# A fused MoE, attention, MoE block on one core: indirect transfers issued without waiting for the pair before, and all engine orders planned anew

## The chip, the cores and the metric

The kernel runs on one core of a Trainium2 chip. The metric is the device time in microseconds (us), taken over several runs. A profile of one execution stands beside it. Its engines are PE (TensorE, matrix products; PEld is its weight load), ACT (ScalarE), DVE (VectorE), POOL (GpSimd) and SP (SyncE, which only issues transfers). An "idle before" in a row is the time in which that engine did nothing ahead of the instruction, with what ended it.

## The reference

The input x has 16 batches of 512 tokens with 128 features, in float32. Three layers follow one another, each on the layer-normalised x and each added to x:

```
x = x + 0.5 * ffn(layernorm(x))     # stage A
x = x + attention(layernorm(x))     # stage B
x = x + 0.5 * ffn(layernorm(x))     # stage C, same weights as A
```

`ffn` is a mixture of 8 experts (128 to 256 to 128, relu between); each token takes its 2 best experts by softmax and adds their results with their softmax weights. `attention` has 8 heads of 32 features, with keys and values through a latent of 64, and a softmax over all 512 tokens of a batch.

## The kernel before

**Stages and steps.** The work is cut into small steps, named by (stage, index, name, number): for example `("C", 12, "xg", 0)`. In stage B the index is a batch, in A and C a batch or a chunk. A chunk is a group of one to three batches that are routed together: chunks 0 to 6 belong to stage A, 7 to 13 to stage C. Chunk 0 (batch 0) and chunk 13 (batch 15) are dense: every expert is computed for every token (`dh`, `dy`), so nothing has to be moved. The other twelve are routed:

- `norm`, `scaled`, `xTf`, `logits`: layer norm, transpose and gate products of a batch; `top1`, `top2`, `rank1`, `gate`, `rank2` choose the experts and compute each token's slot (`pos`, cast on VectorE at L1451).
- `scat` (L1076, GpSimd): for each tile of 128 tokens two indirect transfers, a pair, write the tile's rows to its two slots in DRAM (`slots_A`, `slots_C`). A chunk of three batches has 12 pairs.
- `xload`, `wload` (SyncE) fetch the slots by four tiles (a quad) and each tile's expert weights; `xg` (TensorE, L1657) transposes, `h` and `y` multiply, `ystore` writes to `results`.
- `gat` (L1096, GpSimd): for each tile a pair of indirect transfers brings the two results of every token to `Y`, which has room for two batches; `comb` (VectorE, L1467) adds them to X.

Stage B has for each batch `xT`, `q`, `k`, `v`, and for each of two groups of heads: `rmax` (scores for the maximum and the sums; PE, VectorE L1502, ScalarE L1177), `rsplit`, `mrow`, `s` (transposed scores; ScalarE's exponential at L1168), `pv`; then `wo` adds to X (L1487).

**What sets the order.** Every engine walks a fixed list of steps, in order, and waits at each for the semaphores it needs; a step that waits holds up all that stands behind it on its engine. The lists come from a planner that runs when the program is built (`all_steps`, `plan`): it plays the steps through with a table of costs and picks, whenever an engine is free, the possible step with the smallest due time. The due times are made from a table of numbers (`WANTED`, `B_SHIFT`, `A_SHIFT`, `C_SHIFT` and others). `GAP` is the least distance that the planner puts between the starts of two pairs on GpSimd:

```python
            if step.name in ("scat", "gat") and now < indirect + GAP:
                return False
```

**The wait between pairs.** Before each pair, `apart` waits until the pair ahead of it on GpSimd, scatter or gather, has landed in full. At most one pair is in flight. Besides that, the first scatter of a chunk waits for its slot numbers and for the loads of the chunk before; the first gather of a chunk for the last two stores of results; the first gather of a batch for the combine that frees its half of Y.

The end of the kernel is the routed chunk 12 (batch 14, four pairs out and four back, four quads) beside the dense chunk 13 (batch 15), then the stores of the last batches.

Of the kernel before, what the change touches and what calls it, by code (L numbers as in the profile page):

```python
# [16 lines left out]
TILES, HEADS, GROUP = 4, 8, 4  # L17
# [10 lines left out]
FIRST = tuple(sum(CHUNKS[CHUNKS_OF[s][0]:c]) for s in "AC" for c in CHUNKS_OF[s])  # L28
# [4 lines left out]
W_QUADS, XS_RING, XG_RING, HG_RING, YS_RING, Y_RING, XN_RING, XF_RING, C_RING = 2, 3, 2, 4, 2, 2, 4, 1, 3  # L33
# [10 lines left out]
def n_quads(c):  # L44
    return (n_tiles(c) + 3) // 4
# [36 lines left out]
def split_name(b, g):  # L82
# [4 lines left out]

PERIOD, FIRST_B = 57.89, 143.5  # L90
WANTED = {"norm": -84.66, "scaled": -16.08, "xT": -29.15, ("q", 0): -18.58, ("k", 0): -15.2, ("v", 0): 9.95,
          ("v", 1): -5.64, ("q", 1): 3.68, ("k", 1): 1.22, "wo": 66.92}
GROUP_GAP, MAX_PACE, S_FIRST, S_PACE, PV, ADD, SUM = 18.01, 2.93, 22.06, 0.27, -0.13, -1.26, 4.47
A_LEAD, A_PACE, A_ROUTE, A_NORMS = 40.59, 15.14, 36.72, 8.29
C_NORM, C_ROUTE, C_FIRST, C_PACE, C_GATHER = 63.2, 31.04, 20.92, 29.32, 52.0
LOAD_AHEAD, W_AHEAD = -3.49, -1.76
B_SHIFT = [86.54, -31.84, 6.54, 20.12, -49.35, 18.57, -78.69, -20.22, -54.3, 17.32, 4.45, 0.95, 4.94, -11.17, 16.45, 5.24]
A_SHIFT = [-41.32, -20.34, -9.8, -16.34, 14.33, 47.38, 30.34]
C_SHIFT = [10.17, 7.16, -58.43, 37.75, 10.94, -60.54, 5.88]
GAP = 4.4  # L100


def wanted_attention(b):
# [582 lines left out]
def macaron_kernel(nc, x, wq, wkv_down, wk_up, wv_up, wo, gate_w, gate_b, w1, b1, w2, b2, out):  # L686
# [17 lines left out]
    order = all_steps()  # L704
# [15 lines left out]
    comb_turn = {batch: i for i, batch in enumerate(combs)}  # L720
# [7 lines left out]
    with ExitStack() as ctx:  # L728
# [85 lines left out]
        gy_in = [sem(f"gy_in{i}") for i in range(Y_RING)]  # L814
# [58 lines left out]
        def scattered(s, b):  # L873
            return 32 * TILES * len([old for old in range(b % XN_RING, b + 1, XN_RING) if CHUNK_OF[s][old] != DENSE[s]])
# [11 lines left out]
        def ring_count(i, ring, each=16):  # L886
            return each * (i // ring + 1)
# [114 lines left out]
        def _(pool):  # L1002
# [42 lines left out]
                pool.tensor_tensor(pairs[:, kt // 2, j, :], probs[:, kt - 1, j, :], probs[:, kt, j, :],  # L1045
                                   ALU.add).then_inc(S["p_added"], 1)

            before = {step: old for old, step in zip(order["POOL"], order["POOL"][1:])}

            def apart(at):  # L1050


                old = before.get(at.step)
                if old and old[2] == "scat":
                    s, c, t = old[0], old[1], old[3]
                    b = FIRST[c] + t // TILES
                    pool.wait_ge(scat_in[s][b % XN_RING], scattered(s, b) - 32 * (TILES - 1 - t % TILES))
                if old and old[2] == "gat":
                    i = comb_turn[old[:2]]
                    pool.wait_ge(gy_in[i % Y_RING], ring_count(i, Y_RING, 32 * TILES) - 32 * (TILES - 1 - old[3]))  # L1060

            def scat(at):

                s, c, t = at.stage, at.index, at.k
                apart(at)
                if t == 0:
                    pool.wait_ge(S["pos_done"], at.count("pos_done", "rank2", 0))
                    if c == routed_chunks(s)[0]:
                        pool.wait_ge(zero_in[s], 16)
                    else:  # L1070
                        for q in range(max(0, n_quads(c - 1) - XS_RING), n_quads(c - 1)):
                            i = quad_turn[s, c - 1, q]
                            pool.wait_ge(xs_in[i % XS_RING], ring_count(i, XS_RING))
                b = FIRST[c] + t // TILES
                for k in range(2):
                    pool.indirect_dma_start(out=slots[s][:], out_offset=bass.IndirectOffsetOnAxis(ap=pos[s, c % C_RING][:, k, t:t + 1], axis=0),  # L1076
                                            in_=xn[s][:, xn_place(s, b) + t % TILES, :], in_offset=None).then_inc(
                        scat_in[s][b % XN_RING], 16)

            def gat(at):  # L1080

                s, b, n = at.stage, at.index, at.k
                c = CHUNK_OF[s][b]
                i = comb_turn[s, b]
                apart(at)
                if n == 0:
                    if b == FIRST[c]:
                        for q in range(max(0, n_quads(c) - YS_RING), n_quads(c)):
                            j = quad_turn[s, c, q]
                            pool.wait_ge(y_out[j % YS_RING], ring_count(j, YS_RING))  # L1090
                    if i >= Y_RING:
                        s0, b0 = combs[i - Y_RING]
                        pool.wait_ge(S["comb_done"], counts["comb_done", (s0, b0, "comb", 0)])
                t = (b - FIRST[c]) * TILES + n
                for k in range(2):
                    pool.indirect_dma_start(out=Y[:, i % Y_RING, k, n, :], out_offset=None, in_=results[s, c][:],  # L1096
                                            in_offset=bass.IndirectOffsetOnAxis(ap=pos[s, c % C_RING][:, k, t:t + 1], axis=0)).then_inc(
                        gy_in[i % Y_RING], 16)
# [730 lines left out]
```

## Time and profile before

| | |
|---|---|
| median of 3 runs | 1338.11 us (1331.24 to 1339.2) |
| span of the profiled execution | 1336.0 us |
| its time outside the span | not given by the profile |
| TensorE busy | 1227.4 us |
| ScalarE busy | 962.6 us |
| VectorE busy | 690.4 us |
| GpSimd busy | 470.8 us |

The span goes from the first to the last instruction of that execution, and all times in rows count from its start. A busy time leaves out everything in which an engine waits, whatever it waits for. For GpSimd it holds the time in which it makes the transfers' descriptors, not their flight.

### The profile page before, as it was taken

How to read it: one execution, taken by the hardware profiler on the slowest of the kernel's cores; microseconds unless marked ns; L12 is line 12 of the kernel's file. 1: busy time of each engine (PE TensorE's matmuls, PEld its weight loads, DVE VectorE, ACT ScalarE, POOL GpSimd, SP SyncE). 2: the span in 40 equal slices, each digit the busy share in tenths (PEclk: the TensorE clock that was granted, in tenths of full speed). 3: DMA queues.
4: the chain of work that ended last, by engine and by line, in shares of the span. 5: the costliest groups of instructions: out<-in, count | busy, mean ns of one | idle time of the engine just before them, and what ended most of it. 6: DMA issues, size and time to landing. Idle time of an engine off the chain costs nothing.

```text
span 1336.0 us, 25776 instructions
## 1 busy us (share of the span) xinstructions
PE 1227.4 (92%) x8269; PEld 811.4 (61%) x8269; DVE 690.4 (52%) x2239; ACT 962.6 (72%) x2383; POOL 470.8 (35%) x528
## 2 busy tenths in 40 slices
PE   6989888989999999999999899999799999998795
PEld 2676575576566557666657566667555457665474
DVE  4356446375675446356555365535547546454133
ACT  3338659578788887888887778886778788786331
POOL 2012424434344534234444343433334430243333
PEclk9978999899989998898989989999997879999898
DMA  7305472564645176556445536577421034645672
GB/s 255 141 13 172 145 218 85 175 197 141 190 146 163 48 222 182 160 154 188 132 145 166 150 99 206 166 215 215 147 72 47 31 120 150 195 151 151 206 227 65
DMA packets 159849, 202.04 MB, mean 151 GB/s; under 512 B 16922, under 2 KB 103394, under 8 KB 159715
## 3 DMA queue, kind: packets, MB, share of 16 engines
q1 hardware_dynamic: 144196, 168.90, 41.0%
q0 software_dynamic: 15360, 31.49, 8.1%
q8 instruction: 68, 1.11, 0.4%
q14 instruction: 65, 0.53, 0.1%
q10 hardware_dynamic: 160, 0.01, 0.0%
HBM read 152.49 MB, written 47.84 MB: 150 GB/s over the span
## 4 chain that ended last, share of the span: by engine, by line
DMA 35%; PE 26%; issue 14%; POOL 14%; ACT 7%; DVE 5%; SPq 0%; POOLq 0%; DVEq 0%; ACTq 0%
PE psum L1548 24%; DMA Y<-results_C,posC 10%; DMA slots_C<-xnC,posC 10%; DMA Y<-results_A,posA 8%; POOL Y L1096 7%; DMA slots_A<-xnA,posA 7%; POOL slots_C L1076 4%; ACT psum L1177 2%; POOL slots_A L1076 2%; ACT probs L1168 2%; DVE neg_m L1502 1%; DVE X L1467 1%; ACT xnA L1133 1%; PE psum L1657 1%; PE psum L1625 1%
## 5 line engine op out<-in xcount | busy, mean ns | idle before, releaser
L1548 PE MATMUL psum<-nat 32*128 32x512 f32 x2048 | 413.3, 674 | 17.0 <-ACT psum L1177 8.3
L1502 DVE TENSOR_REDUCE neg_m<-psum 128x1 f32<-128x512 f32 x512 | 318.2, 683 | 202.1 <-PE psum L1548 201.7
L1177 ACT ACTIVATE psum<-psum,neg_m 128x512 f32<-128x512 f32 x512 | 342.8, 692 | 34.5 <-DVE neg_m L1502 33.9
L1168 ACT ACTIVATE probs<-psum 128x512 f32<-128x512 f32 x512 | 267.4, 634 | 45.7 <-PE psum L1548 45.0
L1548 PEld LDWEIGHTS psum<-nat 32*128 32x128 f32 x2048 | 158.5, 193 | 127.0 <-ACT psum L1177 39.2
L1076 POOL DMA_INDIRECT slots_A<-xnA,posA x120 | 117.8, 982 | 255.9 <-DMA slots_A<-xnA,posA 94.6
L1548 PEld LDWEIGHTS psum<-xg_T,wt 128*128 128x128 f32 x1296 | 164.4, 200 | 49.9 <-issue 14.6
L1076 POOL DMA_INDIRECT slots_C<-xnC,posC x120 | 116.4, 970 | 213.0 <-DMA slots_C<-xnC,posC 118.6
L1548 PE MATMUL psum<-xg_T,wt 128*128 128x128 f32 x1296 | 180.9, 290 | 6.6 <-DMA wt<-packed 5.2
L1096 POOL DMA_INDIRECT Y<-results_C,posC x120 | 114.5, 954 | 199.0 <-DMA Y<-results_C,posC 142.0
L1096 POOL DMA_INDIRECT Y<-results_A,posA x120 | 114.8, 957 | 187.7 <-DMA Y<-results_A,posA 128.1
L1548 PEld LDWEIGHTS psum<-wt,hg 128*128 128x128 f32 x1296 | 157.4, 198 | 37.8 <-ACT hg L1210 9.9
L1548 PE MATMUL psum<-wt,hg 128*128 128x128 f32 x1296 | 169.1, 285 | 6.7 <-ACT hg L1210 5.7
L1548 PE MATMUL psum<-m_rows,heads_one 32*128 32x512 f32 x512 | 143.3, 797 | 0.0
L1210 ACT ACTIVATE hg<-psum 128x512 f32<-128x512 f32 (+1 forms) x168 | 97.9, 614 | 48.1 <-PE psum L1548 47.9
L1548 PE MATMUL psum<-probs,V 128*32 128x512 f32 x1024 | 122.3, 619 | 3.8 <-ACT probs L1168 3.7
L1482 DVE TENSOR_TENSOR ys<-psum,wt 128x512 f32<-128x512 f32 x84 | 56.0, 669 | 128.5 <-PE psum L1548 128.3
L1177 ACT ACTIVATION_READ_ACCUMULATOR psum<-psum,neg_m 128x1 f32 x512 | 122.1, 238 | 0.0
L1548 PEld LDWEIGHTS psum<-probs,V 128*32 128x32 f32 x1024 | 33.2, 113 | 74.0 <-issue 61.7
L1189 ACT ACTIVATE o_n<-psum 128x512 f32<-128x512 f32 x32 | 19.3, 604 | 73.1 <-PE psum L1548 73.1
L1238 ACT ACTIVATE xg_T<-psum 128x512 f32<-128x512 f32 x84 | 49.8, 616 | 15.9 <-PE psum L1657 15.8
L1467 DVE SCALAR_TENSOR_TENSOR X<-Y,gateC,X 128x128 f32<-128x128 f32 x120 | 34.3, 348 | 52.0 <-DMA Y<-results_C,posC 51.5
(188 smaller groups left out, 1383.0 us busy)
## 6 DMA issues: line engine op xcount, KB each, us to landing
wt<-packed SPq DMA_DIRECT2D x324, 320.0 KB, 3.9
xs<-slots_A SPq DMA_DIRECT2D x36, 256.0 KB, 4.2
results_A<-ys SPq DMA_DIRECT2D x36, 256.0 KB
xs<-slots_C SPq DMA_DIRECT2D x36, 256.0 KB, 4.4
results_C<-ys SPq DMA_DIRECT2D x36, 256.0 KB
X<-in_L_attn_x_dram SPq DMA_DIRECT2D x16, 256.0 KB, 6.9
out_dram<-X SPq DMA_DIRECT2D x16, 256.0 KB, 2.5
packed<-probs SPq DMA_DIRECT2D x1, 2560.0 KB, 7.8
```

The costliest lines, as they stand in the source:

```text
L1076: pool.indirect_dma_start(out=slots[s][:], out_offset=bass.IndirectOffsetOnAxis(ap=pos[s, c % C_RING][:, k, t:t + 1], axis=0), in_=xn[s][: ...
L1096: pool.indirect_dma_start(out=Y[:, i % Y_RING, k, n, :], out_offset=None, in_=results[s, c][:], in_offset=bass.IndirectOffsetOnAxis(ap=pos ...
L1133: last = act.activation(xn[s][:, xn_place(s, b) + n, :], X[:, b % X_RING, n, :], ACT.Identity, bias=shift[s][:, n:n + 1], scale=rstd[s][:, ...
L1168: act.activation(probs[:, kt, j, :], at.banks()[j][:], ACT.Exp).then_inc(a_done, 1)
L1177: act.activation(at.banks()[j][:], at.banks()[j][:], ACT.Exp, bias=neg_m[:, g, n, j:j + 1], accum_out=sums[:, g, n, j:j + 1]).then_inc(S[" ...
L1189: act.activation(o_n[:, at.k, :], bank[:], ACT.Copy).then_inc(a_done, 1)
L1210: act.activation(hg[:, i % HG_RING, 0:n, :, :].rearrange("p n u t -> p (n u t)"), bank[:, 0:n * UNITS * P], ACT.Relu).then_inc(a_done, 1)
L1238: act.activation(xg_T[:, i % XG_RING, 0:columns], a_bank(at)[:, 0:columns], ACT.Copy).then_inc(a_done, 1)
L1467: last = V_.scalar_tensor_tensor(out=X[:, b % X_RING, n, :], in0=Y[:, i % Y_RING, k, n, :], scalar=gate[s, CHUNK_OF[s][b] % C_RING][:, k, ...
L1482: V_.tensor_tensor(ys[:, i % YS_RING, 0:len(tiles), :], bank[:, 0:len(tiles) * P].rearrange("p (i d) -> p i d", d=D), wt[:, first:first + ...
L1502: V_.tensor_reduce(neg_m[:, g, n, j:j + 1], at.banks()[j][:], AX.X, ALU.max, negate=True).then_inc(S["r_done"], 1)
L1548: return nc.tensor.matmul(dst, w, m, start=start, stop=stop)
```

## The change

`apart` is deleted, with the table that it used, so a pair is issued as soon as its own conditions hold. `GAP` goes from 4.4 to 2.8, and all other numbers of the due-time table are replaced; the planner's rules and its costs of steps are as before. Of that table only three lines are shown.

```diff
-PERIOD, FIRST_B = 57.89, 143.5
+PERIOD, FIRST_B = 60.68, 178.28
...
-C_SHIFT = [10.17, 7.16, -58.43, 37.75, 10.94, -60.54, 5.88]
-GAP = 4.4
+C_SHIFT = [44.98, -107.61, -238.5, 232.44, -10.75, -53.87, 61.72]
+GAP = 2.8
...
-            before = {step: old for old, step in zip(order["POOL"], order["POOL"][1:])}
-
-            def apart(at):
-
-
-                old = before.get(at.step)
-                if old and old[2] == "scat":
-                    s, c, t = old[0], old[1], old[3]
-                    b = FIRST[c] + t // TILES
-                    pool.wait_ge(scat_in[s][b % XN_RING], scattered(s, b) - 32 * (TILES - 1 - t % TILES))
-                if old and old[2] == "gat":
-                    i = comb_turn[old[:2]]
-                    pool.wait_ge(gy_in[i % Y_RING], ring_count(i, Y_RING, 32 * TILES) - 32 * (TILES - 1 - old[3]))
-
             def scat(at):
 
                 s, c, t = at.stage, at.index, at.k
-                apart(at)
...
                 i = comb_turn[s, b]
-                apart(at)
```

The lists of the engines hold the same steps in another order. On TensorE 467 of the 921 steps stand in another place of a line-by-line comparison, on ScalarE 469 of 905, on VectorE 234 of 517, on SyncE 113 of 529, on GpSimd 26 of 240.

GpSimd, the gathers of the last nine routed batches of stage C and what is scattered between them, before (L1076 is a scatter, L1096 a gather, and a pair counts as x2):

```order
L1096 DMA Y<-results_C,posC 128x128 x22
L1076 DMA slots_C<-xnC,posC 3968x128 x24
L1096 DMA Y<-results_C,posC 128x128 x2
L1076 DMA slots_C<-xnC,posC 3968x128 x16
L1096 DMA Y<-results_C,posC 128x128 x22
L1076 DMA slots_C<-xnC,posC 3968x128 x8
L1096 DMA Y<-results_C,posC 128x128 x26
```

And now, where L1061 is the scatter and L1080 the gather:

```order
L1080 DMA Y<-results_C,posC 128x128 x24
L1061 DMA slots_C<-xnC,posC 3968x128 x40
L1080 DMA Y<-results_C,posC 128x128 x24
L1061 DMA slots_C<-xnC,posC 3968x128 x8
L1080 DMA Y<-results_C,posC 128x128 x24
```

The order is nearly the same: one gather of batch 8 goes ahead of the scatters of chunk 10, and the last gather of batch 11 goes ahead of the four pairs of chunk 12.

TensorE, from chunk 11's last products and the attention's last output on, before (`probs,V` is `pv`, `wo_T,o_n` is `wo`, `ident,xs` is an `xg`, `xg_T,wt` an `h`, `wt,hg` a `y`, `ident,xnC` the transpose of batch 15, `xT_F,probs` a `dh` of the dense chunk):

```order
L1548 MATMUL psum<-probs,V 32x512 x16
L1548 MATMUL psum<-xg_T,wt 128x128 x4
L1548 MATMUL psum<-wo_T,o_n 128x128 x8
L1548 MATMUL psum<-xg_T,wt 128x128 x2
L1548 MATMUL psum<-wt,hg 128x128 x6
L1625 MATMUL psum<-ident,xnC 128x128 x4
L1548 MATMUL psum<-gw_T,xT_F 128x8 x4
L1548 MATMUL psum<-xT_F,probs 128x512
L1657 MATMUL psum<-ident,xs 128x128 x4
L1548 MATMUL psum<-xT_F,probs 128x512 x2
L1548 MATMUL psum<-xg_T,wt 128x128 x4
```

And now:

```order
L1532 MATMUL psum<-probs,V 32x512 x16
L1641 MATMUL psum<-ident,xs 128x128 x4
L1532 MATMUL psum<-wo_T,o_n 128x128 x8
L1532 MATMUL psum<-xg_T,wt 128x128 x8
L1641 MATMUL psum<-ident,xs 128x128 x4
L1532 MATMUL psum<-wt,hg 128x128 x8
L1532 MATMUL psum<-xg_T,wt 128x128 x8
L1609 MATMUL psum<-ident,xnC 128x128 x4
L1641 MATMUL psum<-ident,xs 128x128 x4
L1532 MATMUL psum<-wt,hg 128x128 x8
L1532 MATMUL psum<-gw_T,xT_F 128x8 x4
L1641 MATMUL psum<-ident,xs 128x128 x3
```

The first transpose of chunk 12 has moved from behind batch 15's transpose, gate products and a `dh` to right behind the last `pv`, and two of its quads' products now stand ahead of batch 15's gate products.

VectorE, the last steps, before (`ys` is a routed quad, `X<-psum,givenC` a dense `dy`, four instructions each, and `X<-Y` a combine):

```order
L1482 TENSOR_TENSOR ys<-psum,wt 128x384
L1426 SCALAR_TENSOR_TENSOR X<-psum,givenC,X 128x128 x4
L1467 SCALAR_TENSOR_TENSOR X<-Y,gateC,X 128x128 x8
L1426 SCALAR_TENSOR_TENSOR X<-psum,givenC,X 128x128 x16
L1467 SCALAR_TENSOR_TENSOR X<-Y,gateC,X 128x128 x8
```

And now:

```order
L1466 TENSOR_TENSOR ys<-psum,wt 128x384
L1410 SCALAR_TENSOR_TENSOR X<-psum,givenC,X 128x128 x4
L1451 SCALAR_TENSOR_TENSOR X<-Y,gateC,X 128x128 x8
L1410 SCALAR_TENSOR_TENSOR X<-psum,givenC,X 128x128 x16
L1451 SCALAR_TENSOR_TENSOR X<-Y,gateC,X 128x128 x8
L1410 SCALAR_TENSOR_TENSOR X<-psum,givenC,X 128x128 x8
```

After the last routed quad one more dense group follows than before, and the last two dense groups now stand behind the last combine.

Two distances on TensorE are spoken of below. Between `rank2` of chunk 10 and its first `xg` stood 10 `s` and 9 `rmax` with small steps, and now stand 8 and 7. For chunk 7 it was 9 `s`, 8 `rmax` and 8 `h`, and now it is 8 `s` and 7 `rmax` with no `h`.

## Rows read from the trace of the kernel before

**Rows 1.** The page: the span, and each engine's busy time, share and instructions.
```profile
span 1336.0 us, 25776 instructions
PE 1227.4 (92%) x8269; PEld 811.4 (61%) x8269; DVE 690.4 (52%) x2239; ACT 962.6 (72%) x2383; POOL 470.8 (35%) x528
```

**Rows 2.** What GpSimd waited for: us in total, times, longest us.
```profile
POOL Y L1096 <- DMA Y<-results_C,posC: 146.1, 54, 4.9
POOL Y L1096 <- DMA Y<-results_A,posA: 128.1, 44, 5.1
POOL slots_C L1076 <- DMA slots_C<-xnC,posC: 118.6, 54, 5.3
```

**Rows 3.** Timeline, five stops of TensorE, one combine: start us, us, instruction [idle before].
```profile
282.74 0.50 PE L1548 MATMUL psum<-xT_h,wqkv_h 128*128 128x512 f32 x1 [2.55 <-ACT psum L1177]
...
515.67 1.11 PE L1657 MATMUL psum<-ident,xs 128*128 128x128 f32 x4 [2.38 <-ACT psum L1177]
...
760.15 1.18 PE L1548 MATMUL psum<-nat 32*128 32x512 f32 x4 [2.84 <-DVE ys L1482]
...
967.10 1.09 PE L1720 MATMUL psum<-ident,neg_hl 128*128 128x128 f32 x4 [7.07 <-DVE neg_hl L1522]
...
1214.90 1.89 PE L1548 MATMUL psum<-nat 32*128 32x512 f32 x2 [3.90 <-ACT psum L1177]
...
1211.09 2.34 DVE L1467 SCALAR_TENSOR_TENSOR X<-Y,gateC,X 128x128 f32<-128x128 f32 x8 [9.01 <-DMA Y<-results_C,posC]
```

**Rows 4.** Timeline, chunk 12: slot numbers, first and last scatter, TensorE's transposes.
```profile
1235.32 0.42 DVE L1451 CAST posC<-pos_f 128x8 int32<-128x8 f32 x1
...
1247.74 1.01 POOL L1076 DMA_INDIRECT slots_C<-xnC,posC  x1 [3.95 <-DMA Y<-results_C,posC]
...
1264.80 0.96 POOL L1076 DMA_INDIRECT slots_C<-xnC,posC  x1 [0.30 <-issue]
...
1260.91 0.63 PE L1625 MATMUL psum<-ident,xnC 128*128 128x128 f32 x4 [2.97 <-ACT xnC L1133]
...
1270.01 1.09 PE L1657 MATMUL psum<-ident,xs 128*128 128x128 f32 x4 [4.32 <-DMA xs<-slots_C]
```

**Rows 5.** Busy time by stretch; the last three: granted clock, DMA share, GB/s.
```profile
1260.00:1270.00 10.00, 3.95 (x14) 2.21 (x15) 1.34 (x7) 2.19 (x5) 5.57 (x6) 0.64 0.43 144
```

**Rows 6.** Timeline, the last gathers, dense group, combine and stores.
```profile
1310.55 0.95 POOL L1096 DMA_INDIRECT Y<-results_C,posC  x1 [1.82 <-DMA Y<-results_C,posC]
...
1322.62 1.13 DVE L1426 SCALAR_TENSOR_TENSOR X<-psum,givenC,X 128x128 f32<-128x128 f32 x4 [1.55 <-PE psum L1548]
1330.54 2.31 DVE L1467 SCALAR_TENSOR_TENSOR X<-Y,gateC,X 128x128 f32<-128x128 f32 x8 [6.80 <-DMA Y<-results_C,posC]
...
1316.69 16.53 SPq L994 DMA_DIRECT2D out_dram<-X  x3
```

**Rows 7.** Timeline of GpSimd, the first scatters of chunk 10.
```profile
1044.06 1.00 POOL L1076 DMA_INDIRECT slots_C<-xnC,posC  x1 [8.90 <-issue]
1045.36 0.98 POOL L1076 DMA_INDIRECT slots_C<-xnC,posC  x1 [0.30 <-issue]
1047.88 0.97 POOL L1076 DMA_INDIRECT slots_C<-xnC,posC  x1 [1.54 <-DMA slots_C<-xnC,posC]
```

**Rows 8.** All gathers: issue time in ns min/median/max, and us to landing.
```profile
L1096 POOL DMA_INDIRECT Y<-results_C,posC x120: 946/952/1022, 572.8 to 1328.0; - x120
...
DMA to landing us min/median/max: 2.4/3.2/5.8
```

**Rows 9.** DMA queues, the one of GpSimd: packets, MB, share of 16 engines' span.
```profile
q0 software_dynamic: 15360, 31.49, 8.1%
```

**Rows 10.** Timeline of TensorE, chunk 10: rank2 and the first transpose of its slots.
```profile
1039.94 0.47 PE L1548 MATMUL psum<-M,earlier 128*128 128x104 f32 x2
...
1105.86 0.60 PE L1657 MATMUL psum<-ident,xs 128*128 128x128 f32 x4
```

More of the change, by code:

```diff
@@ L83, in split_name @@
     return "rsplit" if by_rows(b, g) else "msplit"
-PERIOD, FIRST_B = 57.89, 143.5
[L91 to L98, printed above, removed]
-C_SHIFT = [10.17, 7.16, -58.43, 37.75, 10.94, -60.54, 5.88]
-GAP = 4.4
+PERIOD, FIRST_B = 60.68, 178.28
+WANTED = {"norm": -92.04, "scaled": 156.81, "xT": -116.69, ("q", 0): 20.83, ("k", 0): -314.6, ("v", 0): 157.44,
+          ("v", 1): 167.85, ("q", 1): -292.35, ("k", 1): -355.47, "wo": 81.64}
+GROUP_GAP, MAX_PACE, S_FIRST, S_PACE, PV, ADD, SUM = 53.54, -6.88, -76.08, 5.15, 22.4, -15.75, 14.15
+A_LEAD, A_PACE, A_ROUTE, A_NORMS = 60.74, 23.89, 15.56, 1.09
+C_NORM, C_ROUTE, C_FIRST, C_PACE, C_GATHER = 68.13, 69.7, 134.52, 14.44, 12.8
+LOAD_AHEAD, W_AHEAD = -15.37, 56.96
+B_SHIFT = [-179.29, 12.49, -70.15, -211.58, -291.63, 108.54, -166.92, -177.62, -134.29, -172.25, 304.35, -178.08, 285.52, -141.14, 159.02, 221.36]
+A_SHIFT = [78.07, -287.7, -223.14, 199.06, 126.67, 186.49, 86.18]
+C_SHIFT = [44.98, -107.61, -238.5, 232.44, -10.75, -53.87, 61.72]
+GAP = 2.8
 def wanted_attention(b):
```

## The prediction

> **What bounds the kernel now.** I read the page first. TensorE is busy for 1227.4 of 1336.0 us (92%), ScalarE for 72%, and GpSimd, which only issues indirect transfers, for 35% [rows 1]. By busy shares the change touches an engine with nothing to do. But busy time leaves waiting out, so the second view is GpSimd's list of waits: its three largest rows are waits for the landing of its own earlier pair, 146.1 + 128.1 + 118.6 = 392.8 us in 152 waits [rows 2]. With its busy time that is 863 us of 1336 before the smaller rows are counted: GpSimd's queue is a long one-at-a-time chain. So the question becomes where that chain ends last, and three other views answer it.
>
> First, TensorE's stops. It runs its list in order, so a late transfer shows as a stop, on TensorE or on the engine that should have emptied a bank. VectorE stands up to 9.01 us at the combine of a batch (L1467) until the gathered rows land, with everything behind it in its list, and TensorE stops in turn: 2.55, 2.38, 2.84, 7.07 and 3.90 us [rows 3]. For each of the five I looked at VectorE in the same microseconds; each time it had just stood at such a combine (at 1211.09 for the last one). The releaser named is ScalarE or another VectorE step, since the wait is handed on. Sum 18.74 us.
>
> Second, the entry of chunk 12 (the last routed chunk). Its slot numbers are cast at 1235.32, but its first scatter goes out at 1247.74, because gathers with their landings stand ahead of it on GpSimd (the row names one as what ended its wait); its fourth pair is issued by 1265.76, and TensorE starts on it at 1270.01 after a stop of 4.32 us, having stopped 2.97 us for the last batch's normalised rows just before [rows 4]. In that stretch TensorE is busy 3.95 of 10 us at a granted clock of 0.64 of full, so between its two levels of 1.2 and 2.4 GHz [rows 5].
>
> Third, the end. TensorE's last product is read by VectorE at 1322.62, but the gathers of the last routed batch begin only at 1310.55, the combine starts at 1330.54 and ends at 1332.85, and the last store is issued at 1333.2; the span ends 2.8 us later [rows 6]. TensorE is done 13.4 us before the end.
>
> **What the change costs and gives.** It removes the wait for the landing of the pair before, ahead of each pair but the first: 239 of 240. It adds no instruction. What still holds a pair back is real: slot numbers, the results' stores, the combine that frees a half of Y. Price of a pair: in the quiet stretch of chunk 10 one scatter takes about 0.97 and the next follows 0.30 behind; the pairs start 3.82 us apart (1044.06 to 1047.88), the second issue's wait of 1.54 included [rows 7]. Without it a pair takes 2 x (0.97 + 0.30) = 2.54 us. In busy stretches the landing itself is late (median 3.2, up to 5.8 us for the gathers [rows 8]), so there a pair loses more than 1.5 us of waiting. No trace shows more than two such transfers in flight. Bounds: 2.5 us (issue alone) and 3.8 us (nothing gained), and in traffic 2.5 to some 6. I take 2.5 to 3: the queue's packets fill only 8.1% of the 16 engines' span, 108 us for 240 pairs, 0.45 us each [rows 9]. So the landing is mostly latency, which overlaps, and not throughput, which wouldn't. The Trainium skill ("DMA: Bandwidth & Descriptors", Anatomy of one DMA) says the same of the fixed two microseconds of a software-issued DMA, that most of it is the write's receipt; the 2.4 us minimum agrees.
>
> Step by step:
> 1. The end. Four gather pairs from 1310.55 to the combine at 1330.54 take 20 us; at 2.5 us a pair and 2.5 us for the landing they take 12.7. Moreover the new order puts more dense work behind the last routed quad: TensorE has six dy steps after it, not five, and VectorE has two dy groups behind the last combine, not none. Then the end is set by the dense batch: VectorE's 1.13 us and 2.8 us of store, with a hop, 4.3 us after TensorE instead of 13.4. Gain 9.1 us. If the gathers are still last, at most 6 of them remain.
> 2. Chunk 12. With its slots ready at 1235.7 and the queue short, four pairs are out by about 1246 to 1250 and the 4.25 us from last issue to first transpose (1265.76 to 1270.01) follows: ready at 1250 to 1254. The new order asks for it right behind the attention's last pv, some 1256 on the old clock, and lays the last batch's transpose behind two of its quads, which covers the 2.97 us. Of 7.29 us of stops I take back 6.
> 3. The five combine stops. A gather pair in traffic saves two to three microseconds and batches come four pairs at a time, so a combine is 8 to 12 us earlier against its chain; the waits of VectorE were up to 9. All 18.7 could go. The new lists are packed against a shorter pair (the planner's gap is 2.8, not 4.4), so some come back. Low end nothing, high end 18.7; I take two thirds, 12.5.
> 4. The clock after stops: a dh step at 1263.64 that the slow stretch doubles, and its neighbours, are worth 2 to 3 us at chunk 12, and a little at the others. I take 3.
> 5. What the tighter order costs. Chunks 7 and 10 now start sooner. For chunk 10 the old list had 19 score and max steps between rank2 and the first transpose, 1039.94 to 1105.86, 65.9 us [rows 10]; the new one has 15, so 52 us. It needs 3 us for the slots, 12 pairs and 4.25 us: at 2.54 a pair 38 us, so it holds. Chunk 7 has 15 as well. Elsewhere the list is repacked in ways that I can't price row by row; for new stops I set 5 us, between 0 and 20.
>
> Sum: 9.1 + 6 + 12.5 + 3 - 5 = 25.6 us off the profiled 1336.0, which is 1310.4. The page gives no time around the span; the runs' median, 1338.11, lies 2.1 over it, inside their spread of 8. Carried over: 1312 us.
>
> **The rivals.**
> *Only the end moves.* Steps 1 and 2 hold, and the combine stops come back in other places, since TensorE and ScalarE are packed at 92% and 72% anyway: 1338 - 15 = 1323. For it: the stops named are only 1.4% of the span. Against: they have a direct cause that goes.
> *Everything gives.* All five stops, all of chunk 12, clock too, and a queue that is half empty lets experts run ahead where attention alone now keeps ScalarE at its pace: 9.1 + 7.3 + 18.7 + 5 = 40, so 1298.
> *Pairs don't get shorter (slower).* With many transfers in flight the issue or the queue itself slows, so that a pair takes as long as before. The place is the start of chunks 7 and 10, where the new order has 52 us: less 7.3 that leaves 44.7 for 12 pairs, so it decides from 3.7 us a pair. At the 4.5 us of a pair in traffic each start is 9.3 us late, and the scatters of chunks 1, 2, 3 and 9 stand closer too, say 5 more; no gain at 1 to 3: 1338 + 9.3 + 9.3 + 5 = 1361, less some microseconds for the better end, 1354. Against: the issue takes 946 to 1022 ns over 120 gathers while VectorE is busy half the time [rows 1, 8]. A rule of the Trainium skill would speak for this rival: "SBUF — State Buffer" (SBUF: two separate sides) has GpSimd locked out from writing descriptors while VectorE copies in its two-port mode. The narrow spread of the issue time doesn't show it here, so I give it no more.
> *No difference.* The new lists, made with other priorities in all five engines, lose in the middle what the end gains: 1335.
>
> **How the numbers follow.** Forecast case (1303 to 1320) 0.50; only the end 0.17; everything gives 0.16; no difference 0.09; slower 0.08. A measurement of this kernel tells about 1% from no change. Within 1% means 1325 to 1351: it takes the no-difference case and a good third of "only the end", 0.16. Slower by over 1%: 0.08. The rest, 0.76, is faster. The range of 8 in 10 leaves out a part of the best case, half of no difference and the slower one: 1294 to 1333.
>
> **What would show it.** In the new profile GpSimd's waits for its own landings are gone and the pairs inside a run start about 2.5 us apart; the issue still takes 0.95 us. The gap from TensorE's last product to the end is 4 to 6 us. The transpose that opens chunk 12 has no stop over 2 us. The sum of VectorE's waits at the combine, now up to 9 us each, falls to a third. Wrong would be: pairs over 3.5 us apart, issue times of 1.5 us and more, TensorE stopped for xs at chunk 7 or 10, or TensorE's busy time up by as much as its stops fall.

## The result, and the profile after

The changed kernel takes 1712.21 us (median of 4 runs, 1711.28 to 1724.54) against 1338.65 us of the kernel before (4 runs, 1331.24 to 1341.69): 1.282 times as long, 95% interval 1.275 to 1.288. The forecast was 1312 us; the range, 1294 to 1333, didn't hold it, and the sign was wrong.

The page's span and engine lines of the changed kernel, and GpSimd's queue:

```profile
span 1711.1 us, 25748 instructions
PE 1322.4 (77%) x8269; PEld 850.1 (50%) x8269; DVE 692.3 (40%) x2239; ACT 964.8 (56%) x2383; POOL 470.1 (27%) x528
...
q0 software_dynamic: 15360, 31.49, 6.1%
```

Against [rows 1] the span is 375.1 us longer, and every engine runs as many instructions as before. TensorE's busy time is 95.0 longer and its idle time, span less busy, goes from 108.6 to 388.7: 280.1 more. ScalarE, VectorE and GpSimd do the same work in the same time. So TensorE waits, and its clock falls while it does (mean granted clock 0.828, before 0.933). Who made it wait? First the waits of GpSimd, which the change was about, then those of TensorE and VectorE (us in total, times, longest):

```profile
POOL Y L1080 <- issue: 308.3, 225, 72.6
POOL slots_A L1061 <- DVE posA L1435: 206.5, 4, 78.6
POOL Y L1080 <- DVE X L1451: 190.4, 8, 52.1
POOL Y L1080 <- DMA results_C<-ys: 159.3, 4, 96.1
```

```profile
PE psum L1532 <- issue: 185.6, 102, 16.6
PE psum L1532 <- ACT nat L1226: 37.8, 2, 34.0
PE psum L1532 <- ACT hg L1194: 36.5, 9, 14.8
```

```profile
DVE neg_m L1486 <- PE psum L1532: 253.9, 83, 49.4
DVE neg_m L1486 <- remote: 227.7, 34, 54.4
```

The waits for GpSimd's own landings [rows 2] are gone, as meant; it is now early everywhere and waits for others. No row of VectorE's waits names a gather any more. TensorE's largest wait is "issue": 185.6 us in 102 pieces for which the profile finds no releaser. VectorE and ScalarE wait for TensorE or for "remote": there a semaphore's update ended the wait, and the profile finds no instruction that ended just before it and could have made it. The program has one core and no partner elsewhere. Over all their rows it is 363.0 us on VectorE and 397.7 us on ScalarE. In the kernel before no wait of either is put down to "remote", so this name serves as a sign below.

The longest such place shows the pattern. GpSimd issues 40 transfers without a stop from 546.4 to 596.9. The timeline of that stretch (start us, us, instruction, idle before):

```profile
553.18 4.34 PE L1532 MATMUL psum<-probs,V 128*32 128x512 f32 x32 [0.43 <-ACT probs L1152]
...
563.56 2.43 PE L1532 MATMUL psum<-nat 32*128 32x512 f32 x4 [0.94 <-issue]
...
595.97 0.95 POOL L1080 DMA_INDIRECT Y<-results_A,posA  x1 [0.30 <-issue]
...
602.88 0.60 ACT L1173 ACTIVATE o_n<-psum 128x512 f32<-128x512 f32 x1 [48.67 <-remote]
604.02 2.09 PE L1532 MATMUL psum<-nat 32*128 32x512 f32 x8 [34.00 <-ACT nat L1226]
606.12 2.48 DVE L1486 TENSOR_REDUCE neg_m<-psum 128x1 f32<-128x512 f32 x4 [49.44 <-PE psum L1532]
```

and the busy time by stretch (columns: us, then PE, PEld, DVE, ACT, POOL, each with its instructions, granted clock, DMA share, GB/s):

```profile
546.00:558.00 12.00, 10.39 (x72) 5.30 (x68) 3.65 (x16) 7.68 (x17) 8.85 (x10) 1.00 0.15 45
558.00:570.00 12.00, 7.96 (x15) 2.62 (x15) 0.00 (x0) 0.00 (x0) 9.26 (x10) 0.62 0.16 55
570.00:582.00 12.00, 0.01 (x1) 0.00 (x0) 0.00 (x0) 0.00 (x0) 9.05 (x10) 0.50 0.14 49
582.00:597.00 15.00, 0.00 (x0) 0.00 (x0) 0.00 (x0) 0.00 (x0) 11.47 (x12) 0.50 0.32 92
597.00:610.00 13.00, 5.98 (x36) 4.14 (x36) 3.08 (x5) 5.83 (x14) 0.00 (x0) 0.55 0.52 154
```

In the first 12 us all engines work. Then ScalarE and VectorE start nothing in three windows, 39 us, and TensorE 15 products in 12 us, 1 in the next 12 and none in 15, at a clock that falls to 0.50, the lower of its two levels (1.2 GHz). Everything resumes six microseconds after the last issue. The `pv` products whose result ScalarE's `o_n` needs started at 553.18 and took 4.34 us; `o_n` starts at 602.88. The DMA engines are busy for a share of 0.14 to 0.32 until the last issue. In the chain of the work that ended last (by engine from the page, and the piece of this stretch) it is one row, and such rows make a fifth of the chain:

```profile
PE 56%; another core or an unknown queue 20%; ACT 12%; issue 7%; DVE 4%; DMA 1%; SPq 1%; ACTq 0%; DVEq 0%
```

```profile
553.63 49.23 another core or an unknown queue
```

Counted over the whole trace: TensorE starts 5.8 products per us outside GpSimd's runs of six and more transfers, and 3.0 inside them (597.8 us in all). There are 34 stretches of over 2.5 us in which none of TensorE, VectorE and ScalarE starts anything, 199 us together; before there were 3, 14 us. I call this the hold.

### The profile page after: what moved, and what is told of

Same layout as the page of the kernel before. It is cut to its first block, busy times and chain, and to the rows that moved or that the text cites. A ratio compares the mean times of both kernels' runs of the same rounds, so it can differ in the third digit from the quotient of the medians.

```text
span 1711.1 us, 25748 instructions
## 1 busy us (share of the span) xinstructions
PE 1322.4 (77%) x8269; PEld 850.1 (50%) x8269; DVE 692.3 (40%) x2239; ACT 964.8 (56%) x2383; POOL 470.1 (27%) x528
## 4 chain that ended last, share of the span: by engine, by line
PE 56%; another core or an unknown queue 20%; ACT 12%; issue 7%; DVE 4%; DMA 1%; SPq 1%; ACTq 0%; DVEq 0%
PE psum L1532 51%; ACT psum L1161 4%; ACT probs L1152 4%; DVE neg_m L1486 2%; PE psum L1641 2%; PE psum L1609 1%; ACT hg L1194 1%; PE psum L1704 1%; ACT xnC L1117 1%; DMA wt<-packed 1%; PE psum L1602 0%; ACT xnB L1117 0%; SPq L977 0%; DMA results_A<-ys 0%
## 5 line engine op out<-in xcount | busy, mean ns | idle before, releaser
L1532 PE MATMUL psum<-nat 32*128 32x512 f32 x2048 | 456.8, 706 | 182.3 <-issue 97.7
L1532 PE MATMUL psum<-xg_T,wt 128*128 128x128 f32 x1296 | 197.7, 302 | 72.9 <-issue 44.7
L1532 PE MATMUL psum<-wt,hg 128*128 128x128 f32 x1296 | 190.3, 305 | 63.2 <-ACT hg L1194 34.8
L1532 PEld LDWEIGHTS psum<-xg_T,wt 128*128 128x128 f32 x1296 | 178.4, 211 | 118.5 <-issue 64.3
L1080 POOL DMA_INDIRECT Y<-results_C,posC x120 | 114.6, 955 | 421.3 <-issue 166.8
L1532 PEld LDWEIGHTS psum<-wt,hg 128*128 128x128 f32 x1296 | 175.9, 216 | 98.4 <-issue 69.0
L1080 POOL DMA_INDIRECT Y<-results_A,posA x120 | 114.7, 956 | 328.2 <-issue 141.6
L1061 POOL DMA_INDIRECT slots_A<-xnA,posA x120 | 116.9, 974 | 278.6 <-DVE posA L1435 206.5
L1061 POOL DMA_INDIRECT slots_C<-xnC,posC x120 | 116.6, 972 | 192.7 <-DVE posC L1435 157.3
L1532 PE MATMUL psum<-probs,V 128*32 128x512 f32 x1024 | 130.2, 646 | 19.7 <-issue 10.0
L1161 ACT ACTIVATION_READ_ACCUMULATOR psum<-psum,neg_m 128x1 f32 x512 | 116.9, 228 | 0.0
L1641 PE MATMUL psum<-ident,xs 128*128 128x128 f32 x324 | 54.6, 299 | 10.3 <-ACT m_rows L1177 5.5
```

Source lines behind the costliest of these rows:

```text
L1161: act.activation(at.banks()[j][:], at.banks()[j][:], ACT.Exp, bias=neg_m[:, g, n, j:j + 1], accum_out=sums[:, g, n, j:j + 1]).then_inc(S[" ...
L1532: return nc.tensor.matmul(dst, w, m, start=start, stop=stop)
L1641: last = nc.tensor.transpose(bank[:, tokens(n)], xs[:, i % XS_RING, n, :], ident[:])
```

## The experiments

The kernels of one group ran on one chip, beside the kernel before; the five groups stood on five chips, which matters further down. Which chip the changed kernel ran on isn't on record. Two parts of the change can be done alone: the waits (`apart`) and the orders (the table with `GAP`).

| | orders | between pairs | median us | ratio, 95% |
|---|---|---|---|---|
| after | new | nothing | 1712.21 | 1.275 to 1.288 |
| *group 1* e1 | new | wait for the pair before | 1546.87 | 1.145 to 1.154 |
| e2 | old | nothing | 1738.84 | 1.288 to 1.297 |
| e3 | old | wait, every 4th pair | 1554.13 | 1.151 to 1.157 |
| e4 | new | wait, every 4th pair | 1548.13 | 1.141 to 1.150 |
| *group 2* e5 | old | pause 1.28 us | 1286.85 | 0.945 to 0.964 |
| e6 | old | wait, every 2nd pair | 1285.40 | 0.944 to 0.962 |
| e7 | old, `GAP` 2.8 | wait | 1548.93 | 1.138 to 1.160 |
| e8 | new, `GAP` 4.4 | wait | 1422.59 | 1.041 to 1.069 |
| *group 3* e9 | new | wait, every 2nd pair | 1360.60 | 1.009 to 1.021 |
| e10 | new | pause 1.28 us | 1381.84 | 1.022 to 1.038 |
| e11 | old | wait, every 3rd pair | 1430.55 | 1.056 to 1.077 |
| e12 | old | pause 0.41 us | 1480.63 | 1.094 to 1.114 |
| *group 4* e13 | old | pause 0.7 us | 1283.06 | 0.946 to 0.964 |
| e14 | old | 2 pauses, every 4th pair | 1290.48 | 0.950 to 0.971 |
| e15 | old | wait, scatters only | 1285.05 | 0.946 to 0.967 |
| *group 5* e16 | old | wait, gathers only | 1551.25 | 1.154 to 1.165 |
| e17 | new | wait, scatters only | 1548.82 | 1.153 to 1.163 |
| e18 | old | 1 pause, every 4th pair | 1647.52 | 1.224 to 1.239 |

**Group 1: waits or orders?** e1 puts `apart` back into the changed kernel, e2 only takes its two calls out of the kernel before:

```diff
-                apart(at)
```

> 

> The changed kernel's orders, with the wait for the pair before put back. Theory S (a long unbroken run of issues on GpSimd holds TensorE up, whatever the order): back near the kernel before, 1320 to 1380 us, TensorE's idle time from 389 us down to 110 to 160. Theory O (the new orders are bad, the waits don't matter): stays at 1650 or more.

> 

> The orders of the kernel before, only the waits between pairs removed. Theory S: as slow as the changed kernel, 1600 to 1750 us, with single stops of TensorE of 10 us and more at the end of runs of 16 and more transfers. Theory O: 1290 to 1340, the prediction's gain or nothing.

e2, with the old orders, is as slow as the changed kernel (1739): taking the waits out does it alone, as theory S said. But e1, with all waits, isn't back at 1338 either: 1547, between its two theories. In e1 it is another loss, as TensorE's and VectorE's waits show; none is put down to "remote":

```profile
PE psum L1657 <- DMA xs<-slots_C: 53.1, 7, 24.2
```

```profile
DVE X L1467 <- DMA Y<-results_A,posA: 173.5, 15, 30.6
DVE X L1467 <- DMA Y<-results_C,posC: 151.9, 15, 24.6
```

These are real releasers: slots that aren't there yet when the new order asks for them, and combines whose gathers come late, 325 us of VectorE's waiting where before had 95.5 (51.5 and 44.0). The new lists count on a pair of 2.8 us and get one of 3.8 and more.

e3 and e4 keep the wait ahead of every fourth pair only, so runs are of eight transfers:

```diff
                 old = before.get(at.step)
+                if turn_of[at.step] % 4:
+                    return
```

> 

> The orders of the kernel before, and the wait for the pair before kept only ahead of every fourth pair, so that at most 8 transfers (10 us) go out in one run. Theory S with a hold-up that builds up with the length of a run (in the changed kernel TensorE starts 5 to 6 products per us in runs of 8, 1.4 to 1.6 in runs of 40): 1310 to 1345 us. Theory F (it is the number of transfers in flight that hurts, from the third on): 1500 or more, since three to four pairs are issued together as before.

> 

> The changed kernel's orders, and the wait only ahead of every fourth pair. Theory S: 1290 to 1350 us; below the kernel before if the planner's shorter distance of pairs is worth what the prediction took it for (25 us). Theory F: 1500 or more.

Both lose some 200 us to the kernel before beside them: eight transfers in a row already hurt. Over e3's 56 runs (nearly all of eight, so 10.2 us) TensorE starts 5.4, 4.8, 2.7, 4.6 and 5.1 products per us in successive 4 us from the run's start, ScalarE 1.5, 1.1, 0.9, 1.7 and 1.5 instructions, VectorE 1.2, 0.8, 0.9, 1.5 and 1.4. The hold reaches ScalarE and VectorE 4 to 8 us in and TensorE after 8 us, and it goes with the run.

The times are those of theory F, its reason isn't. The packets of GpSimd's queue (32 per transfer) show how many transfers are in flight. In the stretch above, from 546.4 to 596.9, the last packet of a transfer ends 1.9 to 2.9 us after its issue starts, and never more than three are in flight; over the whole changed kernel it is at most four. e15 below has up to five and no hold.

**Group 2: must the landing be waited for, and what do the orders cost?** e5 has no landing wait; a fill of 1.28 us on GpSimd stands ahead of each pair. e6 waits ahead of every second pair.

```diff
             def apart(at):
-
-                old = before.get(at.step)
...
+                linked(pool.memset(pairs[:].rearrange("p a b n -> p (a b n)")[:, 0:1400], 0.0))
```

> 

> The orders of the kernel before; instead of the wait for the landing, GpSimd fills 1400 columns of an unused tile with zeros ahead of each pair (some 1.3 us), so pairs start about 3.9 us apart whether they have landed or not. Theory D (what holds the others up is the share of time in which GpSimd issues; 0.50 here against 1.0 without waits): 1320 to 1400 us. Theory L (landings must be waited for; the pause alone doesn't help): 1500 or more.

> 

> The orders of the kernel before, the wait ahead of every second pair, so runs of 4 transfers (5 us). In the runs so far the other engines slow down from 8 us after a run's start. If that onset is a fixed time, runs of 5 us are free: 1300 to 1345 us. If each transfer that isn't waited for costs its share, this lies between 1340 and the 1554 of every fourth pair: near 1450.

Both are 4.6 to 4.7% faster than the kernel before, better than any theory had them. The landing never needed waiting for; a gap in the stream is enough. No kernel of this group has long runs, so the group alone doesn't show that this chip has the hold at all. e9 and e10, on a chip that has it, support the same reading below. e6's page, its GpSimd at chunk 10 (compare [rows 7]) and VectorE at the end (compare [rows 6]):

```profile
span 1284.3 us, 25774 instructions
PE 1211.2 (94%) x8269; PEld 804.3 (63%) x8269; DVE 689.2 (54%) x2239; ACT 961.3 (75%) x2383; POOL 471.7 (37%) x528
```

```profile
1046.09 0.97 POOL L1079 DMA_INDIRECT slots_C<-xnC,posC  x1 [1.53 <-DMA slots_C<-xnC,posC]
1047.36 0.97 POOL L1079 DMA_INDIRECT slots_C<-xnC,posC  x1 [0.30 <-issue]
1048.63 0.96 POOL L1079 DMA_INDIRECT slots_C<-xnC,posC  x1 [0.30 <-issue]
1049.90 0.97 POOL L1079 DMA_INDIRECT slots_C<-xnC,posC  x1 [0.30 <-issue]
1052.40 0.97 POOL L1079 DMA_INDIRECT slots_C<-xnC,posC  x1 [1.53 <-DMA slots_C<-xnC,posC]
...
1278.52 1.13 DVE L1429 SCALAR_TENSOR_TENSOR X<-psum,givenC,X 128x128 f32<-128x128 f32 x4 [1.55 <-PE psum L1551]
1279.56 2.31 DVE L1470 SCALAR_TENSOR_TENSOR X<-Y,gateC,X 128x128 f32<-128x128 f32 x8
```

Two pairs take 6.31 us, 3.2 a pair instead of 3.8. With that all of VectorE's waiting for gathers (95.5 us before) is gone, the last combine stands right behind the last dense group, and the end comes 5.8 us after 1278.52, not 13.4. TensorE idles 73.1 us instead of 108.6 and its granted clock is 0.944 (0.923 to 0.927 in the kernel before on this chip).

e7 and e8 keep all waits and split the table from `GAP`:

```diff
-GAP = 4.4
+GAP = 2.8
```

> 

> All waits kept, the due-time table of before, only the planner's least distance of pairs at 2.8 instead of 4.4. Theory P (an order planned for pairs closer than they can be costs by itself; the changed orders with the waits took 1547): 1400 to 1550. Theory T (the changed due-time table is what costs): 1335 to 1360.

> 

> All waits kept, the due-time table of the changed kernel, the planner's least distance back at 4.4. Theory P: 1340 to 1420. Theory T: 1500 and more, since the table stays.

`GAP` alone, in the kernel before, costs 203 us; with the old `GAP` the new table costs 77. So theory P has e7 right and T wrong, and e8 ends just above P's range: the table costs something too. An order is planned for one length of a pair, and with waits the pair doesn't have it. Neither run has a wait put down to "remote"; 260 us of VectorE's waiting in e7 are for gathers.

**Group 3: how the new orders do once pairs are short, and how much gap is needed.**

> 

> The changed kernel's orders, with the wait for the landing of the pair before put back ahead of every second pair only, so that GpSimd issues at most four transfers (5 us) without a stop. Theory S (unbroken issuing holds TensorE up after some five microseconds, and this was the whole of the loss): pairs now run at about 3.2 us on average, close to what the new orders were planned for, TensorE isn't held up, and the kernel is at or below the like run of the old orders (1285 us): 1270 to 1295. Rival O (the new orders are too tight for any pair slower than 2.6 us, so TensorE stops for slots and combines as it does with all waits, where they cost 203 us): 1380 to 1500.

> 

> The changed kernel's orders with no wait for landings, and a fill of 1.28 us on GpSimd ahead of each pair, so that pairs start 3.8 us apart. Theory S: as a pair takes as long as with all waits in a quiet stretch, but less than with them in traffic, the result is between the run of these orders with all waits (1547) and the like run of the old orders (1287): 1350 to 1450, with TensorE stopped for slots or the transposes' input and not frozen inside runs. Rival O (what matters is only the length of a pair, 3.8 us against 2.54, whatever TensorE sees): 1530 to 1560.

> 

> The old orders, the wait for the landing of the pair before only ahead of every third pair: up to six transfers (7.6 us) without a stop. Runs of four were free (1285 us), runs of eight cost some 210 us (1554). If TensorE is held up from a fixed time after a run's start on, at some 4 to 5 us: 2.5 us of each of up to 80 runs are hit, at half rate, 1370 to 1430. If it sets in by 7 to 8 us (the first landing of the seventh transfer): as with runs of four, 1280 to 1295.

> 

> The old orders, no wait for landings, a fill of about a quarter of the length that was enough (some 0.35 us instead of 1.28) ahead of each pair, so that pairs start about 2.85 us apart and not 3.8. Theory D (any break of the stream of issues lets the other engines through): as fast as with the long fill, 1275 to 1295. Theory R (it is the share of time in which GpSimd issues, or the rate of transfers, that must stay below some limit between 0.67 and 1): most of the loss comes back, 1500 to 1700.

e9 has pairs of about 3.2 us (the new orders were planned for 2.8) and little hold (4 stretches without a start, 22 us), and is 1361 where the old orders gave 1285. So neither expectation held: the new orders cost far less than with all waits, but are not as good. VectorE in e9 still waits for gathers, where e6 had no such row:

```profile
DVE X L1470 <- DMA Y<-results_C,posC: 63.8, 12, 15.2
DVE X L1470 <- DMA Y<-results_A,posA: 45.5, 10, 9.1
```

The hold isn't wholly gone in e9. "remote" ends 35 us of the waits of VectorE and ScalarE there; in e11, on the same chip, it is 203 us, in e10 2.2 us, and in e6 none. Two such rows of e9, then two of e11:

```profile
DVE ys L1485 <- remote: 10.1, 4, 4.9
DVE neg_m L1505 <- remote: 9.2, 5, 5.1
```

```profile
DVE ys L1485 <- remote: 40.5, 10, 8.7
DVE neg_m L1505 <- remote: 38.8, 16, 7.3
```

So runs of four are nearly free on this chip, and a pause of 1.28 us ahead of each pair (e10, with GpSimd busy 56% of the span) is free of the hold but for those 2.2 us.

e10 came out inside the expectation of S. e11, a limit of six, loses 88 us to the kernel before on the same chip, at the top of its first range. In successive 4 us from the start of its 65 runs ScalarE starts 1.8, 1.2, 1.9 and 1.8 instructions per us, VectorE 1.6, 1.0, 1.6 and 1.4, TensorE 6.0, 5.1, 4.9 and 5.7 products: the onset is again 4 to 8 us in. e12 lies between both theories: a break of 0.41 us a pair takes away more than half of what no break costs (138 us are left, where e2 lost 395 on another chip), and not all.

**Groups 4 and 5: a rate, a length, or one kind of transfer?** e13 is e12 with 700 columns instead of 350, e14 has two fills ahead of every fourth pair, e15 and e16 leave out one of the two calls of `apart`, e17 is e15 on the new orders, e18 is e14 with one fill.

> 

> The old orders, no wait for landings, a fill of about 0.68 us on GpSimd ahead of each pair (between the 0.41 us that left 1480 us and the 1.28 us that gave 1287), so that pairs start about 3.2 us apart, the mean of runs of four with a wait (1285). Theory R (a rate: transfers may not be issued faster than one in some 1.55 us on average, however the pauses lie): 1280 to 1310. Theory L (a length: what counts is the number of transfers since the last break of about a microsecond or more): 1400 to 1480, hardly better than with 0.41 us.

> 

> The old orders, no wait for landings, two fills of 1.28 us one behind the other ahead of every fourth pair only: eight transfers without a stop (10.2 us), then 2.6 us of pause, 3.2 us a pair on average. Theory R (a rate over a few tens of microseconds): 1280 to 1320. Theory L (the length of a run is what counts, runs of eight cost over 200 us): 1450 to 1560. In between would say that it is a rate over a time not much longer than a run of four.

> 

> The old orders; the wait for the pair before is kept ahead of the scatters (SBUF to DRAM) and taken away ahead of the gathers (DRAM to SBUF). Taking both away cost 450 us against the same kernel with pauses (1739 against 1287). If both kinds of transfer hold TensorE up alike: about half of it, 1450 to 1570. If it is the writes into SBUF by the gathers alone: 1650 to 1750. If it is the scatters alone (their scattered writes to DRAM): 1280 to 1340.

All three of group 4 land at 1283 to 1290, and in none of them does a single stretch of 2.5 us pass without a start or "remote" end a wait. Read alone, e13 and e14 are theory R, and e15 says that gathers do no harm. Group 5 forbids both readings.

> 

> The complement of the run with the scatters' waits kept (1285 us): old orders, the wait for the pair before kept ahead of the gathers and taken away ahead of the scatters. With both away the kernel took 1739, with the scatters' waits alone kept nothing was lost. If unbroken scatters are what does the harm: 1500 to 1739, TensorE nearly stopped in the runs of scatters. If either kind alone is harmless and only both together hold TensorE up: 1280 to 1310.

> 

> The changed orders with the waits put back ahead of the scatters only; gathers issue without a stop. Theory S (what matters is that the scatters are spaced; the new orders cost 75 us even with short pairs): no hold, scatter pairs of 3.8 us and gather pairs of 2.5, so between the run with a wait every second pair (1361) and the one with a pause a pair (1382): 1350 to 1400. Rival T (these orders hang runs of scatters and gathers together, so TensorE is held up again): 1450 to 1600.

> 

> The old orders, no landing wait, one fill of 1.28 us ahead of every fourth pair instead of two: runs of eight transfers with a break about as long as that of the landing wait of the run with waits every fourth pair (1554 us); with two fills it was 1290. Theory B (the length of the break, so the mean rate, decides; here 2.86 us a pair): 1480 to 1570. Theory K (the kind of break decides: a fill lets the other engines through, a wait for a landing doesn't): 1285 to 1310.

e16: scatters alone, unbroken, cost 213 us. e17: gathers alone, unbroken, hold TensorE too, 1549 against the 1350 to 1400 without a hold. And e18 is slower than e3, though its break is a fill: theory K falls, and B is only right in direction. Now compare two runs of 16 gathers by busy time, columns as above. e15, from 559.6 on:

```profile
559.00:563.00 4.00, 4.00 (x37) 2.76 (x35) 0.61 (x1) 3.12 (x7) 2.79 (x3) 1.00 0.97 310
563.00:567.00 4.00, 4.00 (x34) 1.68 (x27) 0.08 (x1) 0.75 (x2) 2.97 (x4) 1.00 0.82 229
567.00:571.00 4.00, 4.00 (x33) 2.18 (x32) 0.17 (x1) 3.20 (x7) 2.90 (x4) 1.00 0.96 288
571.00:575.00 4.00, 4.00 (x35) 3.12 (x35) 4.00 (x7) 3.70 (x11) 3.09 (x4) 1.00 0.37 113
```

e17, from 680.4 on, GpSimd quiet for 98 us before it:

```profile
680.00:684.00 4.00, 4.00 (x35) 1.27 (x27) 3.79 (x20) 3.58 (x11) 2.91 (x3) 1.00 0.89 246
684.00:688.00 4.00, 2.33 (x18) 1.17 (x16) 0.38 (x2) 0.00 (x0) 2.93 (x3) 1.00 0.58 193
688.00:692.00 4.00, 0.00 (x0) 0.00 (x0) 0.00 (x0) 1.67 (x5) 3.03 (x4) 0.89 0.19 49
692.00:696.00 4.00, 0.00 (x0) 0.00 (x0) 1.98 (x3) 0.00 (x0) 3.09 (x4) 0.50 0.19 50
```

The same instruction, the same 1.26 us apart, a long quiet ahead of both (35 us in e15), more DMA traffic in the one that is free: and one is held and the other isn't. I took all runs of eight or more transfers with over 15 us of quiet ahead and counted TensorE's starts 6 to 11.5 us in. In e14 and e15 there are 6.7 per us (11 and 5 runs, none under 4.0). In the changed kernel, e2, e3, e4, e16, e17 and e18 there are 2.4 to 3.4 (6 to 25 runs each). What a run does to the other engines is thus not set by how the run is issued alone. The number in flight isn't it either: by their queue's packets, up to five in e14 and e15, up to four in e17. Group 4 stood on one chip and the held kernels of groups 1, 3 and 5 on three others, so the nearest candidate is a difference between chips; but no kernel with long runs was run on two of them. It wasn't tried, and stays open. (The kernel before, with runs of two, had medians of 1338 to 1346 in all groups.) Therefore e13 to e15 can't be set against e12, e3 and e2, and whether the limit is a length or a rate isn't settled either. Within one chip it is ordered by breaks: in group 1, 1739 with none, 1554 with one per eight; in group 3, 1481 with 0.41 us per pair and 1431 with a wait per six transfers.

## Why the prediction was wrong

**Where it failed.** The step is "What the change costs and gives": it priced the unbroken issuing on GpSimd alone and put its cost to the other engines at nothing, without a reason. Its price of a pair, "I take 2.5 to 3", and the reason that the landing is "mostly latency, which overlaps" are both true as far as GpSimd goes: pairs start 2.5 us apart (first scatters of chunk 12, compare [rows 4]),

```profile
1599.04 1.01 POOL L1061 DMA_INDIRECT slots_C<-xnC,posC  x1 [14.93 <-DVE posC L1435]
1600.35 0.99 POOL L1061 DMA_INDIRECT slots_C<-xnC,posC  x1 [0.30 <-issue]
1601.64 0.97 POOL L1061 DMA_INDIRECT slots_C<-xnC,posC  x1 [0.30 <-issue]
```

and landings keep coming every 1.27 us, some 2.2 us behind their issue, with no queue building up. What the step left out is that the price of a transfer may be paid by engines that have nothing to do with it. "No trace shows more than two such transfers in flight" looked for the risk in the wrong number: the transfers in flight stay few, and what is new is a stream of issues with no break in it. The hold is worth some 356 us: the changed kernel loses 374 to the kernel before, e9 (the same orders, runs of four) 18.

**The rival that came nearest** was the slower one, which put the harm on the issue or the queue (pairs no shorter, 1354). Its sign was right and its mechanism wrong: the issue takes 947 to 1072 ns over all gathers, nearly as in [rows 8]. The Trainium skill's rule in "SBUF — State Buffer" (SBUF: two separate sides), on GpSimd locked out by VectorE, doesn't show in these issue times either.

**Point by point.** Step 1, the end: held. In the changed kernel VectorE's last dense group starts at 1707.55 and the span ends 3.6 us later; 13.4 us became 3.6, forecast 4.3. Step 2, chunk 12: its first scatter leaves 0.4 us after the slots are cast (1598.6), and no wait for xs is among TensorE's waits any more. Step 3, the combines: VectorE's waits for gathers went to nothing, not to a third; in e6, with the old orders, likewise. Their size was set too low: I counted five stops of TensorE, 18.7 us, but e6 gains 60 us on the kernel before (1285.4 against 1345.6 beside it), more than the 40 of "everything gives". Between the two profiles, 51.7 us apart, TensorE's idle time is 35.5 us less and its busy time 16.2 less. That the part beyond the stops I listed is VectorE's waiting, passed on in small pieces, is argued and not shown. Step 4, the clock: it goes with the stops, in e6 up (0.944, against 0.923 to 0.927 beside it), in the changed kernel down (0.828, TensorE's busy time up 95 us). Step 5, the tighter order, "I set 5 us, between 0 and 20": wrong by far. With pairs as long as before the new orders cost 203 us (e1), with pairs of 3.2 us still 78 (e9 against e6, some hold included), and with a pause ahead of each pair 98 (e10 against e5), nearly all without a hold. These two are across chips. I had checked the starts of chunks 7 and 10 and not the combines.

**The sum as the runs give it.** Each kernel is set against the kernel before beside it. Shorter pairs, old orders: 1285.4 - 1345.6 = -60 (e6). New orders at that pair length: e9 is at +18, so +78. The last breaks taken away: the changed kernel is at +374, so +356. The three come from different chips, and e9's +18 still holds a little of the hold, so the last two are rough.

**What would have shown it.** "Wrong would be TensorE's busy time up by as much as its stops fall": busy time and stops went up together, a case not on the list. The list held only ways in which the change might miss its aim, none in which it hit it and something else broke.

## What to carry to other kernels

A wait that looks like waste can be the only thing that spaces a stream; before you take it out whole, take out half. Here, in the old orders, waits ahead of every second pair (at most four indirect transfers, 5 us, in a row) gave 4.7% (0.944 to 0.962), and none at all lost 29% (e2). Long runs did no harm in group 4 for a reason that isn't known, so don't count on it.

When waits named "issue" or "remote" grow on several engines of a one-core program at once, look at what another engine is doing without a stop.

An order planned for one transfer time can cost more at another than it gains (203 us in e7): change the planned gap and the real one together, and measure each alone.

## What the runs showed of the hardware

While GpSimd issues indirect transfers without a break, TensorE, ScalarE and VectorE slow down and can come to a stand: ScalarE and VectorE 4 to 8 us in, TensorE after 8 us over e3's runs and from 4 us on in the stretch of e17. It happens in every kernel with runs of six or more outside group 4, and in e12 with breaks of 0.41 us between pairs ("remote" ends 228 us of waits there), whether the transfers are scatters (e16) or gathers (e17), with the DMA engines at a share of 0.14 to 0.32 in the changed kernel's longest stretch. Semaphore updates of DMA transfers go on through it, and SyncE issues on (at 583.19 and 591.61). TensorE's updates come late: six products that end between 557.5 and 570.0 by the profile have their updates between 602.86 and 603.11. GpSimd merely busy does no harm: in e10, on a chip with the hold, it is busy 56% of the span, with fills between pairs. What is held up, the updates or the products, and by what part of GpSimd's work, isn't shown. It isn't the fetching of instructions in the stretch above: TensorE goes on at 604.02 with no fetch between 554 and 618. The Trainium skill, "DMA: Bandwidth & Descriptors" (SWDGE vs HWDGE vs iDMA), says that GpSimd's descriptors for such transfers go to rings in an SBUF carveout. No run here shows whether that has a part in the hold.
